# Attention on one core: TensorE's output products between the two score products of a pair

## The reference, cut to what matters

```python
q = (queries @ Wq + bq).reshape(N, L, H, D)      # N=16, L=64, H=16, D=16
k = (keys @ Wk + bk).reshape(N, S, H, D)         # S=1601
v = (values @ Wv + bv).reshape(N, S, H, D)
sm = jnp.einsum('nlhd,nshd->nlhs', q, k) / math.sqrt(D)
sm = jax.nn.softmax(sm, axis=1)                  # over the queries l, for each key s and head h
attn = jnp.einsum('nlhs,nshd->nlhd', sm, v).reshape(N, L, H * D)
return attn @ Wo + bo
```

## Time and profile before

| what | value |
|---|---|
| median of three runs | 1540.8 us |
| span of the profiled execution, first to last instruction | 1519.6 us |
| attention, in the profile | about 31 to 684 us of the span |
| PE matmul, busy share of the whole span | 88% |
| PE weight load | 66% |
| DVE | 85% |
| ACT | 77% |
| POOL | 73% |

### The profile page before, as it was taken

The page is one execution under the profiler, slowest core; times in us unless marked ns, Lnnn a source line. Parts: engine busy times, 40 slices in busy tenths (PEclk is TensorE's granted clock), DMA queues, the critical chain, the costliest instruction groups (busy, mean ns, idle before and its releaser), DMA issues. The chain is left out here.

```text
span 1519.6 us, 34485 instructions
## 1 busy us (share of the span) xinstructions
PE 1339.1 (88%) x12560; PEld 1001.5 (66%) x12560; DVE 1291.7 (85%) x1894; ACT 1163.9 (77%) x2975; POOL 1107.2 (73%) x1092
## 2 busy tenths in 40 slices
PE   5999999999999999978777777777777899999995
PEld 5888888888888888755333333333333678888884
DVE  4899999999999999987699999999999645666664
ACT  5888888888888888754699999999999235555552
POOL 2988888888888888754299999999999351443431
PEclk9999999999999999999899999999999999999998
DMA  4223131111111111005654110200000026888994
GB/s 135 59 74 103 45 85 49 39 46 38 46 44 38 48 42 31 2 2 132 163 89 80 17 32 1 35 14 1 2 1 1 1 68 261 311 303 308 307 310 139
DMA packets 106866, 132.99 MB, mean 88 GB/s; under 512 B 43274, under 2 KB 97617, under 8 KB 103256
## 3 DMA queue, kind: packets, MB, share of 16 engines
q1 hardware_dynamic: 96872, 61.61, 16.7%
q0 software_dynamic: 9840, 69.36, 12.8%
HBM read 110.47 MB, written 14.49 MB: 82 GB/s over the span
## 5 line engine op out<-in xcount | busy, mean ns | idle before, releaser
L565 POOL TENSOR_TENSOR half<-prob 128x512 f32<-128x512 f32 (+1 forms) x208 | 266.9, 1283 | 91.8 <-ACT prob L602 89.4
L597 ACT ACTIVATE prob<-ps_s,mx 128x64 f32<-128x64 f32 (+1 forms) x1040 | 239.1, 339 | 98.5 <-DVE prob L708 98.5
L1372 DVE TENSOR_TENSOR state<-ps_u,state 128x1024 f32<-128x1024 f32 x252 | 297.3, 1219 | 7.1 <-POOL state L1235 3.1
L701 DVE TENSOR_REDUCE mx<-ps_s 128x16 f32<-128x1024 f32 (+1 forms) x208 | 253.0, 1216 | 13.8 <-PE ps_s L648 12.3
L1330 PE MATMUL ps_y<-state,cz 128*32 128x256 f32 x2048 | 247.8, 384 | 1.8 <-DVE zs L1352 1.0
L648 PE MATMUL ps_s<-qbd,kT 64*128 64x256 f32 (+1 forms) x1664 | 221.1, 395 | 14.7 <-ACT prob L597 12.7
L708 DVE TENSOR_TENSOR prob<-ps_s,mx 128x192 f32<-128x192 f32 (+3 forms) x416 | 198.4, 518 | 7.2
L648 PEld LDWEIGHTS ps_s<-qbd,kT 64*128 64x128 f32 (+1 forms) x1664 | 147.8, 182 | 67.1 <-issue 38.5
L1330 PEld LDWEIGHTS ps_y<-state,cz 128*32 128x32 f32 x2048 | 109.1, 110 | 106.3 <-issue 30.0
L1312 PE MATMUL ps_u<-x_rows,b_diag 48*128 48x256 bf16 x1024 | 79.4, 275 | 112.0 <-DVE state L1372 105.0
L602 ACT ACTIVATE prob<-prob 128x704 f32<-128x704 f32 (+1 forms) x208 | 173.8, 836 | 0.0
(11 more groups left out here) (263 smaller groups left out, 3413.2 us busy)
## 6 DMA issues: line engine op xcount, KB each, us to landing
raw<-in_ctxT_dram SPq DMA_DIRECT2D x80, 268.0 KB, 2.8
x_rows<-ssm_x SPq DMA_DIRECT2D x96, 64.0 KB
raw<-in_ctxT_dram SPq DMA_DIRECT2D x16, 261.0 KB, 2.8
b_diag<-blank SPq DMA_DIRECT2D x2, 2048.0 KB, 8.9
slot_rows<-blank SPq DMA_DIRECT2D x1, 3483.0 KB, 15.4
xg<-slot_rows SPq DMA_DIRECT2D x27, 128.0 KB, 4.9
ssm_x<-xp SPq DMA_DIRECT2D x6, 384.0 KB, 3.9
back<-y_slots SPq DMA_DIRECT2D x8, 256.0 KB, 4.5
```

The source lines that it names most:

```text
L565: pool.tensor_tensor(half[0:rows, :, :], prob[0:rows, g % SLOTS, :, 0:L // 2], prob[0:rows, g % SLOTS, :, L // 2:L], ALU.add).then_inc(hal ...
L597: ins = nc.scalar.activation(prob[0:rows, g % SLOTS, h, :], part[:, h, :], ACT.Exp, bias=mx[0:rows, g % 2, h:h + 1])
L701: nc.vector.tensor_reduce(mx[0:rows, g % 2, :], part, AX_X, ALU.max, negate=True)\
L1372: nc.vector.tensor_tensor(h, flat(ps_u[k % 2][:, :, :]), h, ALU.add).then_inc(state_ready, 1)
```

## The change

In TensorE's loop the block of `outputs_of(i)` is moved from the end of the turn to a place between `scores(2i)` and `scores(2i+1)`. No instruction is added or taken away and no other engine's program is edited. In turn i the order becomes: first scores, outputs of pair i-2, second scores, key and query products, values of pair i-1. In the last three turns, which have no scores, the outputs now stand ahead of the values.

```diff
             for i in range(PAIRS + 3):
                 if i < PAIRS:
                     scores(2 * i)
+                for g in outputs_of(i):
+                    outputs(g)
+                if i < PAIRS:
                     scores(2 * i + 1)
                     for kind, n, j in jobs_of(i):
                         job(m, kind, n, j)
                         m += 1
                 if 1 <= i <= PAIRS:
                     values(i - 1)
-                for g in outputs_of(i):
-                    outputs(g)
```

## The result

The changed kernel takes 1603.9 us (median of 4 runs, 1600.6 to 1609.4) against 1540.6 us (1539.8 to 1541.1): 1.042 times the time, interval 1.040 to 1.044, 63.3 us more. The ratios further down, with their intervals in brackets, are likewise against the kernel before, timed beside each kernel. The forecast was 1600.3 us in a range of 1574 to 1622.

A forecast was written before the change was run, and what follows sets the result against it. VectorE was taken to bound the attention, TensorE just behind: 22.5 + 1.6 + 34.3 = 58.4 us, 47.5 after 10.9 of existing waits, 59.5 with the clock. 1540.8 + 59.5 = 1600.3 us, range 1574 to 1622.

The forecast's parts named there:

- VectorE's bound of 5.96: Attention: VectorE's own ordinary turn, `vn` to `vn`, takes 5.96 us and bounds it, TensorE's 6.01 only just behind.
- Moved instructions: TensorE's turn: moving outputs between the scores changes its blocks' time by -0.2 to +0.3 us a turn, taken as 0.
- Its cover: Ordinary turns: the 6.26 cycle against TensorE's 6.01 hides longer blocks; past that 0.25 the rest would cost 4 us.
- the new cycle of 6.26: Ordinary turns: `vn` hand-over 0.15, outputs 1.01, second scores to maximum 1.18, to next `vn` 3.92; 22.5 us over 75 turns.
- The last sentence of the prediction: Attention: the reasoning is wrong if second maxima don't wait, outputs start well over 0.2 behind `vn`, or first maxima wait more.
- Turns with one tile: Straddling pairs, 8 turns: cycle 5.82 under VectorE's own, but late first scores cost 0.20 each, 1.6 us.
- Turns with `take_output`: 15 item ends: outputs wait for the masked copy, 8.72 or 9.16 us against 6.76; 34.3 us in all.
- The sum without the clock: Attention: 22.5 + 1.6 + 34.3 = 58.4 us over VectorE's own 596.1.
- The clock: `take_output` turns: TensorE idles some 2.7 us, 15 times, so its clock falls; eight falls that cost, 12 us.
- The rival that the clock holds: Attention: the idle stretches bring no fall of TensorE's clock, giving 1588.3 us; chance 0.20.
- The base: Whole kernel: the runs' median lies 21.2 us above the profile's span of 1519.6, left as it is.
- The tail: Very end: values stand behind outputs, at most one block of 1.01, but GpSimd's sums end last; cost 0.

The follow-up runs named there:

- e9: Changed kernel with outputs of pair i-3, masked copy at the head of VectorE's turn, one of three key-split products left out: 1540.0 us, 1.0002.
- e10: Kernel before the change with one of the three products of the key split left out: 1525.6 us, 0.9908.
- e8: Changed kernel with the masked copy at the head of VectorE's turn and one of three key-split products left out: 1548.7 us, 1.0052.
- e4: Changed kernel with outputs of pair i-3 instead of i-2 and the masked copy at the head of VectorE's turn: 1554.1 us, 1.0092.
- e6: Changed kernel with outputs of pair i-3 instead of i-2, masked copy left in its place: 1605.4 us, 1.0427.
- e3: Changed kernel with second scores' products issued twice more ahead of the outputs at the 15 item ends, filling TensorE's stall: 1586.0 us, 1.0322.
- e5: Changed kernel with the masked copy (`take_output`) moved ahead of the first softmax part in VectorE's turn: 1555.7 us, 1.0097.
- e7: Changed kernel with one output tile between the scores, the rest behind the values; turns with an item's first tile in old order: 1566.5 us, 1.0167.
- e0: Kernel before the change, unchanged, run and profiled once more: 1537.2 us, span 1535.5.
- e2: Changed kernel with outputs between the scores only in the 15 turns holding an item's first tile, elsewhere behind the values: 1601.3 us, 1.0412.
- e1: Changed kernel, but in the 15 turns whose outputs hold an item's first tile they stay behind the values: 1554.0 us, 1.0107.

## Why the prediction was right or wrong

**VectorE's bound of 5.96: right.** e9 and e10 run at it.

**Moved instructions, taken at 0: this step failed.** "I bound the difference at -0.2 and +0.3 a turn and take 0, as each block keeps its kind of neighbour change." The scores did not keep theirs: they had stood next to each other, and that neighbour was the cheap one. In the medians of after, start to start: first scores 1.06, outputs 1.01, second scores 1.06, key products 1.60, values 1.51, in all 6.24 against 6.01. The difference is 0.23, inside the bounds, but not the 0 that was taken. Of it 0.20 is the two score blocks (2.13 against 1.93 where they adjoin); the rest is that the one turn of the earlier trace rows was a little short, as key products and values take 1.60 and 1.51 in the medians of before too. The moved outputs take 1.01 in either place.

**Its cover failed with it.** "What hides it is the new cycle of 6.26 below against 6.01": the cycle measured 6.18 (e8), because the hand-over from `vn` is 0.05, not 0.15. So TensorE's 6.24 ends last, by 0.06, and the cycle alone sets only the 8 ordinary turns that follow a turn without key or query products (6.17). Ordinary turns took 6.24 in the mean, where the cycle had given 6.26; the sum came out (468.2 against 469.5 us for 75 turns) for a wrong reason: that was luck. The last sentence of the prediction named the sign: in the other 67 turns the first maxima wait (0.20 in the mean) and the second don't (0.00). e4 and e6 show what the wrong reason costs: I removed the cycle and expected a gain that a second limit, 0.06 away, held back.

**Turns with one tile: 6.16 predicted (5.96 + 0.20), 6.22 measured**, by the late first scores, as told (the first maxima stand idle 0.21); 0.5 us over the 8.

**Turns with `take_output`: right.** With the clock held (e3) 9.16 as predicted for three tiles, 9.09 against 8.92 for two, in all 35.5 over VectorE's 6.76 where 34.3 was said. e5 shows that the masked copy's place is the cause.

**The sum without the clock: right.** 596.1 + 58.4 = 654.5; e3 has 654.7.

**The clock: mechanism right, size off.** After's 673.1 less e3's 654.7 are 18.4 us, against the 12 taken: 11 falls in the granted clock, not eight, at 18.4 / 11 = 1.67 instead of 1.51. All eight three-tile ends fell and three of the two-tile ends. The rival that the clock holds is out. By the Trainium skill (TensorE: Matmul & The Clock Gate, Why this matters for your kernels), which warns only of longer gaps than these, it would have held; the falls behind 2.88 us here and behind 2.07 in e7 speak against that, and the measurement decides. The prediction read its own rows of before too closely: the granted clock was still 1.00 from 38.04 to 39.12 and from 732.72 to 735.44, so the falls came 1.1 and 2.7 us behind the stretches of 1.86 and 2.24, the second one after two more stretches of 0.54 and 0.60.

**The base: wrong, without effect.** "the median of the runs lies 21.2 above the span": 1.7 lie there, and the rest comes of the wait in the experts that e0 has and the first profile lacks. As both sides of a difference share it, it cancelled.

**The tail: about right.** From the last `vn` of the 98 turns to the last masked copy after takes 6.68 us, before 6.28 and e0 6.62. The stretch from there to the state space block's first step differs by some 3 us from execution to execution (78.5 before, 77.5 e0, 80.1 after, 77.4 e3), without an order that goes with the edits.

## What to carry to other kernels

Where two engines are within a few per cent of each other, add up both turns after a change of order, each block measured with the neighbour that it will have; a block that loses a like neighbour can be dearer, and one limit removed only shows the next. Before a product is moved to an earlier place on an engine that works in order, look for what it waits for at that place on the other engine: here a copy of 0.41 us, behind 2 us of other work, cost 53 of the attention's 66 us with the clock's falls, and moving that copy ahead gave 52 back (673.1 to 621.3). When a stall on TensorE costs more than its length, compare the granted clock behind it; filling the stall with work that nobody needs tells the two apart.

## What the runs showed of the hardware that was not expected

**A score block alone costs more.** 1.06 us from its start to a block of another kind, 0.97 in a run of two. e7 has the same for outputs: 0.57 and 0.58 for single tiles, 1.01 for two. The starts of the single matmuls place the extra time: inside a block of scores one pair of matmuls follows another by 0.21, but the second pair of a block starts 0.31 behind the first, and the next block of another kind 0.31 behind the last pair. Two blocks in a row have this longer step once at each end, two blocks apart twice: about 0.10 + 0.10 more. What the engine does in it stays open.

**Two hand-overs.** From the end of `vn` to the first matmul that waited for it 0.05 us pass (239.43 to 239.48 in e8, and the same in 72 of its 75 ordinary turns), under the 0.15 taken from the earlier trace rows. That 0.15 was no stray value: behind the masked copy it is 0.15 at all 15 ends of after. So the price read at one instruction did not hold for another on the same two engines; why they differ stays open.

**Equal stalls, unequal clocks.** In after an idle stretch of 2.74 us left the clock up, its outputs took 1.08 (the stretch from 311.60 above):

```profile
311.75 1.08 PE L672 MATMUL ps_o<-prob,vn 128*32 128x128 f32 x32 [2.74 <-DVE otmp L737]
```

In e2 an idle stretch of 2.74 at the same place was followed by a fall, and the same outputs took 1.94:

```profile
315.47 1.94 PE L672 MATMUL ps_o<-prob,vn 128*32 128x128 f32 x32 [2.74 <-DVE otmp L742]
```

In after alone seven stalls were 2.74 us long, and the clock fell at three of them. Shorter ones did it too, as in a turn of e7 that is followed by scores at 2.04 instead of 1.13:

```profile
385.45 0.65 PE L672 MATMUL ps_o<-prob,vn 128*32 128x128 f32 x16 [2.07 <-DVE vn L728]
386.02 2.04 PE L648 MATMUL ps_s<-qbd,kT 64*128 64x256 f32 x8
```

All four such stalls of e7 were followed by a fall, but of four of 2.06 in e1 only one, and of seven of 1.78 in e9 two; the 1.99 of e5 held. The fall came between 1.0 us before and 0.9 us behind the end of the stall in after. So the length of the stall doesn't settle it by itself; what else does stays open.

**Waits of 15 us that come and go.** The "remote" entry of e0 and after, 20.3 us in two waits in the experts, is missing in the first profile of the same program alone. What it waits for the profile doesn't name. A single span isn't to be compared with another one below that size; the turns of one stage can be.
